# The seam between dispatch and combine of a soft mixture of experts: the last softmax sum and the last root on VectorE, expert rows loaded in two parts

## The reference

```python
logits   = einsum('bmd,dnp->bmnp', x, phi)            # 64 experts x 32 slots
dispatch = softmax(logits, axis=0)                    # over the 16 sequences
combine  = softmax(logits.reshape(b, m, n*p), axis=-1)
slots    = einsum('bmd,bmnp->bnpd', x, dispatch)
y        = einsum('bnpd,nde->bnpe', slots, W) + b[None, :, None, :]
out      = einsum('bnpd,bmnp->bmd', y, combine)
x        = layernorm(x + out)
```

## Time and profile before

| what | value |
|---|---|
| median of 3 runs | 1579.81 us (1579.48 to 1579.84) |
| time of the profiled execution | 1580.04 us |
| its span, first to last instruction | 1578.1 us |
| mean granted TensorE clock | 0.974 |
| PE busy | 91% of the span |
| DVE, ACT, POOL busy | 77%, 52%, 50% |
| dispatch, its regular part | 1096 to 1362 us |
| between dispatch and combine | 1362 to 1401 us |
| combine, its regular part | 1403 to 1569 us |

### The profile page before, as it was taken

One profiled execution on the slowest core, in us unless ns is written; L12 is line 12 of the kernel. 1 busy time (PEld: TensorE's weight loads), 2 busy tenths in 40 slices (PEclk: granted clock), 3 DMA queues, 4 the chain that ended last, 5 costly groups with the idle time before them and its releaser, 6 DMA issues. The chain is left out here.

```text
span 1578.1 us, 32322 instructions
## 1 busy us (share of the span) xinstructions
PE 1438.5 (91%) x10752; PEld 1261.2 (80%) x10752; DVE 1214.6 (77%) x2335; ACT 820.8 (52%) x1846; POOL 790.4 (50%) x1959
## 2 busy tenths in 40 slices
PE   5588999999999999999999999946999999869997
PEld 4366788788788788788788787836999999869997
DVE  4466798898898898898898887764888888736664
ACT  2234544544544544544544544303777776557774
POOL 0332253553553553553553552222777777557763
PEclk9998999999999999999999999966999999989999
DMA  6000000000000000000000000008676667877782
GB/s 236 7 7 1 8 1 14 15 1 14 15 1 15 15 1 14 15 1 15 15 1 15 8 1 8 8 7 252 171 197 188 185 186 199 254 266 301 300 316 71
DMA packets 140752, 132.10 MB, mean 84 GB/s; under 512 B 7376, under 2 KB 130512, under 8 KB 134096
## 3 DMA queue, kind: packets, MB, share of 16 engines
q1 hardware_dynamic: 140624, 130.50, 26.1%
HBM read 73.85 MB, written 56.62 MB: 83 GB/s over the span
## 5 line engine op out<-in xcount | busy, mean ns | idle before, releaser
L636 PE MATMUL bk<-ve_f,oe 128*128 128x128 f32 x2048 | 275.8, 279 | 0.8 <-DVE ve_f L1360 0.8
L636 PEld LDWEIGHTS bk<-ve_f,oe 128*128 128x128 f32 x2048 | 248.9, 192 | 23.4 <-issue 20.1
L2287 POOL TENSOR_TENSOR d_s<-d_ex 128x1024 f32<-128x1024 f32 x32 | 131.8, 4120 | 100.8 <-ACT d_ex L2087 100.8
L1360 DVE SCALAR_TENSOR_TENSOR ve_f<-ps_m,oT 128x512 f32<-128x512 f32 x248 | 166.3, 678 | 3.7 <-PE bk L636 2.3
L1321 DVE COPY_PREDICATED vals<-oh,bk 128x1024 f32<-128x1024 int32 x112 | 146.6, 1309 | 10.3 <-PE bk L404 8.5
L2037 PE MATMUL d_sl<-d_ex,e_prT 128*128 128x128 f32 x1024 | 136.0, 277 | 8.8 <-POOL d_ex L2304 8.8
L1971 PE MATMUL d_lg<-d_phf,d_xtf 128*128 (+1 forms) x1024 | 128.1, 287 | 14.4 <-DVE d_ex L2191 7.6
L1971 PEld LDWEIGHTS d_lg<-d_phf,d_xtf 128*128 128x128 f32 x1024 | 125.1, 203 | 15.2 <-issue 11.1
L2037 PEld LDWEIGHTS d_sl<-d_ex,e_prT 128*128 128x128 f32 x1024 | 125.4, 193 | 9.0 <-POOL d_ex L2304 9.0
L1981 PE MATMUL d_sl<-d_ex,d_xs 128*128 128x128 f32 x1024 | 121.3, 277 | 5.8 <-DVE d_ex L2202 5.8
L1981 PEld LDWEIGHTS d_sl<-d_ex,d_xs 128*128 128x128 f32 x1024 | 118.4, 194 | 6.2 <-DVE d_ex L2202 6.2
(11 more groups left out here) (340 smaller groups left out, 3730.5 us busy)
## 6 DMA issues: line engine op xcount, KB each, us to landing
logits<-d_raw SPq DMA_DIRECT2D x128, 256.0 KB, 3.3
e_lt<-logits SPq DMA_DIRECT2D x32, 1024.0 KB, 5.1
y_slots<-d_ys SPq DMA_DIRECT2D x64, 256.0 KB, 4.3
d_ex<-y_slots SPq DMA_DIRECT2D x16, 1024.0 KB, 6.8
d_w<-W SPq DMA_DIRECT2D x16, 256.0 KB, 3.4
oe<-xT SPq DMA_DIRECT2D x1, 2048.0 KB, 7.9
xt_in<-xT SPq DMA_DIRECT2D x16, 128.0 KB, 2.3
x_in<-x SPq DMA_DIRECT2D x16, 128.0 KB, 2.4
```

Of the source, the lines that this page charges most:

```text
L636: last = pe.matmul(ps_u[:, cols], oe[:, hp, e, :], mo[:, n % MO, hp, :], start=False, stop=(e == NE - 1 and hp == HP - 1), skip_group_chec ...
L1360: V.scalar_tensor_tensor(mo[:, n % MO, :, :].rearrange("p a n -> p (a n)"), chosen_of(b, c), float(NE - e), oT[:, u, c, :, :].rearrange("p ...
L2287: G.tensor_tensor(s8[:], part[:, 0:8, :], part[:, 8:16, :], ALU.add).then_inc(n, 1)
```

## The change

The four additions of the last softmax sum (g = 31) move from POOL to DVE, where they stand directly behind the `scaled` of g = 30, and `greatest(0, 0, 0, 0)` moves behind the last `scaled`. On ACT `weights(0, 0, 0)` moves ahead of the last four `outputs`, and `weights(0, 0, 1)` into the middle of the first four `turned`. The last `newton` (batch 15) moves from POOL to DVE. The expert rows of batches 0 and 1 get a buffer of their own (`e_y01`), so that only batches 2 and 3 (and every later one with v = 2 or 3) lie in `d_ex`. For batches 0 to 3 the rows of blocks 0 to 13 are loaded from DRAM as soon as their stores have landed (`load_early`, 128 x 1792 elements, 0.92 MB), and the rows of blocks 14 and 15 are copied from `d_ys` by DMA (`copy_late`: four DMAs for each batch and block, 32 partitions by 512 bytes each, so 32 DMAs in all). The bias of batch 0 is added in three pieces. Semaphores that nothing waited for are dropped.

```diff
@@ soft_experts
-        yb = ex[:, :, :, :, :, :].rearrange("p u c k b s -> p (u c) (k b) s")
+        y01 = sb("e_y01", [2, SB, D])
+        yb = [y01[:, v, :, :] for v in range(2)] + [ex[:, 0, c, :, :, :].rearrange("p k b s -> p (k b) s")
+                                                   for c in range(C)]
+        EARLY = SB - 2
+        LATE_IN = [16 * 2 * XB, 16 * 2 * XB * (YB - 1)]
@@ SP
+            def load_early(b):
+                sp.dma_start(yb[b][:, 0:EARLY, :].rearrange("p s e -> p (s e)"),
+                             y_dram[b * (XB * NS):(b + 1) * (XB * NS), 0:EARLY * D]).then_inc(loads[b], 16)
+            def copy_late(s, b):
+                for j in range(XB):
+                    sp.dma_start(yb[b][j * NS:(j + 1) * NS, s, :], ys[0:NS, s % 2, b, j, :]
+                                 ).then_inc(y_late[1 if b else 0], 16)
             for u in range(2):
-                store_y(SB - 2 + u, u)
+                sp.wait_ge(stores[u], Y_STORES - 16 * BB)
+            for b in range(2):
+                load_early(b)
+            store_y(SB - 2, 0)
+            copy_late(SB - 2, 0)
+            sp.wait_ge(q["slot1_ps"], BK * (SB - 1))
+            for b in range(2, YB):
+                load_early(b)
+            for b in range(1, YB):
+                copy_late(SB - 2, b)
+            for b in range(YB):
+                sp.wait_ge(q["ys"], BK * (SB - 1) + b + 1)
+                copy_late(SB - 1, b)
+            store_y(SB - 1, 1)
             for u in range(2):
                 sp.wait_ge(stores[u], Y_STORES)
-            for b in range(YB):
-                load_y(b, b)
@@ PE, weigh
-                if c == 0 and k % 2 == 0:
-                    pe.wait_ge(e["y"], 2 * b + k // 2 + 1)
+                if isinstance(b, int) and b == 0:
+                    if c == 0 and k == 0:
+                        pe.wait_ge(q["ys"], BK * SB)
+                    if c == 0 and k != 1:
+                        pe.wait_ge(e["y"], k if k else 1)
+                elif c == 0 and k % 2 == 0:
+                    pe.wait_ge(e["y"], 2 * b + k // 2 + 2)
@@ ACT
-            for k in (2, 3):
+            weights(0, 0, 0)
+            for k in range(BK):
                 outputs(SB - 1, 1, SB // 2 - 1, k)
-            weights(0, 0, 0)
+            turned(0, 0, (0, 1))
             weights(0, 0, 1)
-            turned(0, 0, range(BK))
+            turned(0, 0, (2, 3))
@@ DVE
+            def summed(g, u, c):
+                n, k = q["sum"], 4 * g
+                part = ex[:, u, c, :, :, :].rearrange("p k b s -> p (k b) s")
+                dve.wait_ge(n, k)
+                dve.wait_ge(q["ex"], 2 * (g + 1))
+                V.tensor_tensor(s8[:], part[:, 0:8, :], part[:, 8:16, :], ALU.add).then_inc(n, 1)
...
+            summed(C * SB - 1, 1, 1)
+            scaled(C * SB - 1, 1, 1)
             greatest(0, 0, 0, 0)
-            scaled(C * (SB - 1) + 1, 1, 1)
@@ DVE, end
             residual(NB - 1, 1, 1)
+            newton(dve, wait_apart, e["rstd"], RSQRT_OPS * (NB - 1), (e["moments"], 2 * C * NB),
+                   mv[:, 1, :, 1], 1.0, EPS, v, h, y[:, 1, :], t)
             norm(NB - 1, 1, NB // 2 - 1)
@@ POOL
+            pool.wait_ge(loads[0], W_LOADS + 16)
+            add_bias(0, slice(0, SB // 2))
+            add_bias(0, slice(SB // 2, EARLY))
+            pool.wait_ge(y_late[0], LATE_IN[0])
+            add_bias(0, slice(EARLY, SB))
+            for v4 in range(1, YB):
+                pool.wait_ge(loads[v4], (W_LOADS if v4 < 2 else 0) + 16)
+                add_bias(v4, slice(0, SB // 2))
+                pool.wait_ge(y_late[1], LATE_IN[1])
+                add_bias(v4, slice(SB // 2, SB))
```

More of the change, by code:

```diff
@@ L290, in token_blocks @@
         q = {n: sem(n) for n in names}
-        norms = {n: {k: sem(f"{n}_{k}") for k in ("moments", "rstd", "rows")}
-                 for n in ("rms", "ln1", "ln2", "lnB", "lnC", "lnD")}
+        norms = {n: {k: sem(f"{n}_{k}") for k in ("moments", "rstd", "rows")} for n in ("ln1", "lnB", "lnC")}
+        norms.update({n: {k: sem(f"{n}_{k}") for k in ("moments", "rstd")} for n in ("ln2", "lnD")})
+        norms["rms"] = {"rstd": sem("rms_rstd")}
         nbuf = {n: (sb(f"{n}_st", [C, 6]), sb(f"{n}_mv", [C, 2]), sb(f"{n}_v", [C]), sb(f"{n}_h", [C]),
@@ L1823, in soft_experts @@
         bias_in = sem("e_bias_in")
+        y_late = [sem(f"e_y_late{n}") for n in range(2)]
         l_in = [[sem(f"e_l_in{u}{c}") for c in range(C)] for u in range(2)]
@@ L1884, in load_y @@
                 wait(sp, e["out_ps"], C * (b - YB + 1))
-                sp.dma_start(yb[:, v, :, :].rearrange("p s e -> p (s e)"), y_dram[bass.ds(b * (XB * NS), XB * NS), :]
+                sp.dma_start(yb[v].rearrange("p s e -> p (s e)"), y_dram[bass.ds(b * (XB * NS), XB * NS), :]
                              ).then_inc(loads[v], 16)
+            def load_early(b):
[5 more added lines that the diff above has]
+                                 ).then_inc(y_late[1 if b else 0], 16)
             def store(b, u):
@@ L2036, in weigh @@
                     s = 4 * k + j
-                    last = pe.matmul(po[:, c, :], prT[:, c, s, :], yb[:, v, s, :], start=(s == 0), stop=(s == SB - 1),
+                    last = pe.matmul(po[:, c, :], prT[:, c, s, :], yb[v][:, s, :], start=(s == 0), stop=(s == SB - 1),
                                      skip_group_check=True)
@@ L2058, in _ @@
                     block_of(pair, u)
-            block_of(SB // 2, 0, now=False)
             for k in (2, 3):
+                experts(SB - 2, 0, SB // 2 - 1, k)
+            for c in range(C):
+                for k in range(BK):
+                    slots(SB - 1, 1, c, k)
+            for k in range(BK):
                 experts(SB - 1, 1, SB // 2 - 1, k)
@@ L2159, in _ @@
                     block_of(pair, u)
-            block_of(SB // 2, 0, now=False)
-            for k in (2, 3):
+            outputs(SB - 2, 0, SB // 2 - 1, 2)
+            outputs(SB - 2, 0, SB // 2 - 1, 3)
+            for k in range(BK):
+                slots(SB - 1, k)
+            weights(0, 0, 0)
+            for k in range(BK):
                 outputs(SB - 1, 1, SB // 2 - 1, k)
-            weights(0, 0, 0)
+            turned(0, 0, (0, 1))
             weights(0, 0, 1)
-            turned(0, 0, range(BK))
+            turned(0, 0, (2, 3))
             for v in range(YB):
@@ L2298, in block_of, with add_bias @@
                     summed(C * s + c, u, c)
+            def add_bias(v, rows):
+                G.tensor_tensor(yb[v][:, rows, :], yb[v][:, rows, :], bias[:, rows, :], ALU.add).then_inc(e["y"], 1)
             def biased(b, v, q4):
@@ L2302, in biased @@
                 for half in range(2):
-                    rows = slice(SB // 2 * half, SB // 2 * (half + 1))
-                    G.tensor_tensor(yb[:, v, rows, :], yb[:, v, rows, :], bias[:, rows, :], ALU.add
-                                    ).then_inc(e["y"], 1)
+                    add_bias(v, slice(SB // 2 * half, SB // 2 * (half + 1)))
             def moments(b, u):
@@ L2314, in _ @@
             block_of(1, 1)
-            with pool.Fori(1, SB // 2) as pair:
+            with pool.Fori(1, SB // 2 - 1) as pair:
                 for u in range(2):
                     block_of(2 * pair + u, u)
+            block_of(SB - 2, 0)
+            summed(C * (SB - 1), 1, 0)
             pool.wait_ge(bias_in, 16 * XB)
-            for w4 in range(YB):
-                biased(w4, w4, 0)
+            pool.wait_ge(loads[0], W_LOADS + 16)
[8 more added lines that the diff above has]
+                add_bias(v4, slice(SB // 2, SB))
             for w4 in range(YB):
@@ L2327, in _ @@
                     biased(YB * four + w4, w4, four)
-            for w4 in range(YB):
+            for w4 in range(YB - 1):
                 moments(NB - YB + w4, w4 % 2)
```

6 lines of the change are left out of this document (added).

## The result

The kernel became slower, a little: 1585.16 us (1582.28 to 1586.71) against 1579.82 us (1579.48 to 1581.66), six runs of each. The ratio is 1.0029 with the interval 1.0016 to 1.0042, so the loss of 0.29% is above the 0.2% that can be told from no change, though the interval begins just under it. In a second comparison, of 5 rounds, the medians were 1583.80 and 1579.97 and the ratio 1.0028 (1.0016 to 1.0040). The forecast of 1574.5 and its range of 1567.5 to 1581 both missed.

The account below looks back on a forecast made before the run. PE was taken to bound the regular combine, its start set by waits at the dispatch's end. Gains of 3.5 by batch 1's end and 1.8 in the tail, 5.3 off 1580.04, gave 1574.7, median 1574.5; 8-of-10 range 1567.5 to 1581.

Parts of the forecast that it names:

- the price of a copy: SP's queue in front of the stores of block 15: 0.48 per copy issue, 15.4 for all 32.
- The bounds of 0.37 to 0.76: SP's queue: lowest and highest time from one copy issue to the next, around the 0.48 taken.
- the break-even: SP's queue: `load_l(2, 0, 0)` at 1407.7, or 0.65 per copy; beyond it SP is later than PE's own progress before.
- slower: SP's queue: 0.76 per copy and stores held up to 1380.1, load at 1412.0, time 1584.1; chance 0.12.
- eaten up: SP's queue: copy issue 0.55 to 0.65; with 0.585 the load goes out at 1406.4, time 1578.5; chance 0.16.
- SP's queue is late next, and PE stalls in the middle of batch 1 for logits.: Combine: fifth logit load at 1402.4, 8.1 later; PE idles about 5; batch 1 ends at 1418.7, gaining 3.5, not 16.6.
- The last `slots` at 1372.6, at full clock.: End of the dispatch on PE: matmuls begin at about 1372.6 instead of 1375.9, clock held; PE can enter batch 0 at 1384.3.
- The last store's issue ends at 1379.5.: SP's queue, block 14: issue of the last store ends between 1376.8 and 1380.1, taken as 1379.5.
- Stores of block 15 to the fifth load 6.6.: SP's queue: from first issue of block 15's stores to all landed 6.6, so `load_l(2, 0, 0)` is issued at 1402.4.
- The stall in batch 0 costs nothing.: PE in batch 0: last bias comes around 1394, wanted at 1388.7; the wait lies inside batch 1's stall, costing nothing.
- The tail: Kernel's end on DVE: last aggregate to last rows shortened, 1.8 gained, bounds 1.6 and 1.9.
- The fixed part for each DMA.: SP's copies: about 2 us each, overlapping; rival paid one after another at 1.65: load at 1440, time 1612; chance 0.02.

Follow-up runs that it names:

- the probe: Kernel before plus seven series of eight small DMAs behind its last store; issue medians 0.59 or 0.60 with both ends on chip; total time not compared.

## Why the prediction was wrong

**The step that failed is the price of a copy**: "An issue with nothing to wait for begins 15.53 - 15.05 = 0.48 after the one before it", "that row is for transfers with about as little to describe, and I take it: 15.4". They took 22.9. From the first copy at 1378.83 to the stores of block 15 at 1402.80 it is 23.97, less 1.10 for the two early loads between them. Of the 7.5 too much, 32 x (0.63 - 0.48) = 4.8 is the price of an issue with both ends on chip. The first four, issued right behind the stores while the queue was full, took 4.39 instead of 4 x 0.63 = 2.52, 1.9 more. The rest, 0.8, is a short wait for the rows of block 15 (0.4) and one longer issue (1.07). The bias loads with a median of 0.585, which I left to a rival, were nearer by their number, but they come from DRAM too. In the program each reads one row into 32 partitions, which none of the probe's does; whether that is why they cost more was not tried. No row of before had a transfer with both ends on chip, and I chose among DRAM's prices by the number of pieces. The bounds of 0.37 to 0.76 did hold it.

**Price and hold-up together decide the sign.** The forecast named the break-even: the fifth load at 1407.7, or 0.65 per copy. The load went out at 1409.66, and the copies cost 22.9 / 32 = 0.71 each with the hold-up in them. The 4.8 of the price alone would have put the load at 1407.2, just short of break-even; the 1.9 at the first four carries it over. From there the arithmetic of the forecast holds: load + 16.3 gives 1426.0, as measured. The rival "slower", at 0.12, was the right one, the copies held up behind the four stores included. The rival before it, "eaten up", had its number wrong: 32 times 0.585 puts the load at 1405.8, and with the 0.05 to the next issue at 1407.4, not at 1406.4, so its price and the break-even were hardly apart. Put into the sum, the measured load and tail give 1580.04 + 3.8 - 1.4 = 1582.4, against 1582.28.

The other steps:
- *SP's queue is late next, and PE stalls in the middle of batch 1 for logits.* Right; 8.19 in place of 5. That of the copies only SP's issue time counts was also right: the median copy lands 2.2 after its issue, and they overlap.
- *The last `slots` at 1372.6, at full clock.* 1371.22, which with the 1.24 of the mark is 1372.5; clock 1.00. PE in batch 0 at 1384.3: 1382.63, with the 1.24 1383.9. Right, and worth nothing: putting the sum back on POOL left the time where it was.
- *The last store's issue ends at 1379.5.* 1378.78, though the hold-up was larger than taken: one issue of 8.16 and one of 1.48. Counted from the mark it is 0.5 later than forecast.
- *Stores of block 15 to the fifth load 6.6.* 6.86.
- *The stall in batch 0 costs nothing.* It was 9.17 in place of some 5, with the clock at 0.50 behind it, and it still lay inside the other. It isn't harmless: its cause, the late biases, is what the kernels without the logits' stall wait for. With the logits moved ahead, PE waited 4.17 behind those biases.
- *The tail, 1.8, "with no doubt about its place".* The place was right, the size 1.4. The fifteen instructions took 1577.56 - 1574.42 = 3.14, not 2.84, and 0.11 passed before them. L65 begins 0.28 behind L63 and L72 only 0.19 behind L70 in the rows above; earlier in the kernel the same fifteen had fitted into 2.84.

**The fixed part for each DMA.** The Trainium skill, DMA: Bandwidth & Descriptors, section Anatomy of one DMA, has about 2 us for it, and the prediction took that as a rule for SP's DMAs. The section gives its figure for DMAs that GpSimd issues, and says that most of it is the time until the write is confirmed. Paid one after another it would have given 64 for the copies; they were issued in 22.9 and overlapped, so the low chance of that rival, 0.02, was fair. The advice to join small DMAs was right here for a reason that shows in SP's rows: joined by two, they brought the ratio from 1.0029 to 0.9956.

**What stays open.** Runs of the changed kernel scatter more (4.4 between the fastest and slowest of six, and 5.7 of eleven) than those of before in the first comparison (2.2 of six), though in the last one those of before did as well (6.9 of 21). The profiled one is the fastest of its six, and no trace shows what a run of 1586 does otherwise; the mark at the end of the dispatch moves by up to 4.7 between executions, and where that comes from stays open. A kernel whose copies are issued by another engine's queue was not tried, nor was one with the biases in another order on POOL.

## What to carry to other kernels

Count what is queued on the DMA-issuing engine between a wait and the next load that somebody needs, and price each issue: here 32 copies took 22.9 us of issue, and the wait that they were to remove was 8.80. Price an operation by a row with the same kinds of ends; if there is none, measure it by itself before choosing, above all where the two ends of the bound lie on different sides of the break-even. Join copies before moving them: here the issue cost the same for twice the bytes. And try the parts of a change apart: the sum and the root alone gained about 5 us, which is what the whole change was to gain.

## What the runs showed of the hardware that I had not expected

- Issue of a DMA on SP: 0.59 to 0.60 us with source and target both on chip (4, 16 and 64 KB), 0.42 to 0.43 with one of them in DRAM (16 and 64 KB), for 32 and 128 partitions alike; some 0.05 more to the next. The bias loads of the earlier trace rows, at 0.585 from DRAM, show that another form of transfer can cost more.
- While the DMA engines are full (busy share 1.01 from 1369.1 to 1377.3), SP is held up in whatever it issues next: 8.16 us in one store's issue, and 2.25 in that of the copy of 16 KB that follows the stores.
- `TENSOR_SCALAR` of 128x128 on DVE, 0.60 for two, took 4.67 beside two `TENSOR_TENSOR` of 128x1024 on POOL; POOL's own were no slower for it (2.34 each, 2.37 on average over the kernel before).
